# Linear attention in 64-key tiles: the running state takes up a chunk's early keys ahead of its late queries

## The chip, the cores and the metric

The kernel runs on one core of one Trainium2 chip. The metric is the device time of one execution in microseconds (us).

## What is computed

The input is x of shape (16, 512, 256) in float32. Two blocks follow each other, each with a residual. The attention block is causal linear attention with 16 heads of 64 columns:

```python
x = x + attn(layernorm(x))        # Wq, Wk, Wv: 256 x 1024, Wo: 1024 x 256
x = x + ffn(layernorm(x))         # fp4 rounding in blocks of 16 of inputs and weights

q = relu(x @ Wq) + 0.001;  k = relu(x @ Wk) + 0.001;  v = x @ Wv      # per head
context = cumsum(k_n outer v_n)                     # over the positions n, 64 x 64 a head
attn_n = (q_n @ context_n) / (q_n . cumsum(k)_n)
out = attn @ Wo + bo

h = silu(fp4(x) @ fp4(w_gate)) * (fp4(x) @ fp4(w_up));  y = fp4(h) @ fp4(w_down)
```

Since the sum over positions is causal, a block of queries needs the scores q.k of its own block, masked, times v, and q times the state that the keys before the block have left. The denominator comes out of the same products: v has a 65th column of ones.

## The kernel before

A sequence has 4 chunks of 128 tokens, c = 0 to 3; two chunks make a half u. Everything is software-pipelined by chunk: step g = 4b + c handles the attention of chunk g, the gate and up products of chunk g - 2 and the down product of chunk g - 3. Each engine has its queue written out by hand in `step(b, c)`, and engines wait for each other by semaphores only. Heads come in 8 pairs; the heads of a pair lie on partitions 0 to 63 and 64 to 127 of `qkT`. Pairs 0 to 3 are half 0, pairs 4 to 7 half 1.

TensorE's step, in order: in even chunks `turn_x` (transposes of the next half's normalized x); `scores`; `turn_k` (k to token-major, for chunks 0 to 2); `turn_xq`; `project_v` for the next half (six pairs of 512-column matmuls); `attend`; `update_state` (chunks 0 to 2); in odd chunks the first half of `project_qk` for the next half of the sequence, with `turn_hq(0)` and `turn_hq(1)` (transposes of the rounded hidden rows, 4 and 2 of them) between; in even chunks the two `turn_hq` alone; then twice `gate_up` and `turn_attn`; in odd chunks the rest of `project_qk`; `down`; `project_out`.

The projections use float32r operands split in a high and a low part (`product`, L408). The attention products are plain float32, and each shows in the profile as two matmuls. In `scores` the early 64 keys of a pair meet all 128 queries (L473, 64x64 tiles, 128 columns) and the late 64 keys the late 64 queries (L479, 64 columns). In `attend` come the state's products (L514, 64x64, 65 columns, not in chunk 0), early queries by early keys (L527, 64x64) and late queries by all 128 keys (L535, 128x64 tiles). `update_state` (L548) adds the chunk's 128 keys to a pair of PSUM banks (128x64 tiles). Chunk 3 updates no state.

VectorE's step up to the attention: in even chunks `low_x` (L1049, L1075); mask 0 of four (L1188, 128x384 each, scores times the causal mask into `probs`); `variance` of the second layer norm of chunk g - 1, which GpSimd turns to a shift and ScalarE to `xn2` (L849); masks 1 to 3; `begin_x`: amax, scale, inverse and scaled x (L1080 to L1089), which waits for `xn2`; `low_xq`; in odd chunks `round_h(g - 3)` (two ops on 704 columns); `end_x` (L1094, L1096), which waits for ScalarE's square of x; then `normalize(0)` and `normalize(1)` (L1220, L1222), each when its half of the attention is in PSUM; `add_state` (L1208 or L1210), when `update_state` is done; `low_hq`, and so on.

ScalarE's step: in even chunks `high_x`; `xn2` (L849); two evacuations of k to `k_tok` (L854); `xqT_hi` (L838); the square of x (L863); two evacuations of v (L702); then the hidden rows, silu and so on.

The 8 PSUM banks go round. `keys` lists the uses of a period of four chunks in a fixed order; the n-th use gets bank n mod 8, and an entry "none" fills up where an av or kv pair would be split. Ahead of each use, `Banks.take` makes TensorE wait for the semaphore with which the bank's last user's reader let it go: v by `v_ready` (ScalarE's evacuation), av by `attn_ready` (normalization), kv by `state_ready` (the addition of the state), wo by `x2_ready`. The core of it:

```python
spread = []
for key in keys:
    if key[0] in ("av", "kv") and key[2] % 2 == 0 and len(spread) % 8 == 7:
        spread.append(("none", len(spread), 0))
    spread.append(key)
bank_of = {**in_turn(first, 8), **in_turn(spread, 8)}
```

In the first steps the FFN weights are quantized and turned as eight jobs at places of `JOBS_AT`, through banks of `W_BANKS`.

Of the kernel before, what the change touches and what calls it, by code (L numbers as in the profile page):

```python
# [5 lines left out]
ALU = mybir.AluOpType  # L6
# [7 lines left out]
P = 128  # L14
# [40 lines left out]
def build_program(nc, x, Wq, Wk, Wv, Wo, bo, w_gate, w_up, w_down, out):  # L55
# [25 lines left out]
    with ExitStack() as ctx:  # L81
# [37 lines left out]
        probs_banks = sb("probs", [P, 4, 6 * DH])  # L119
# [48 lines left out]
        scores_done, probs_ready = sem("scores_done"), sem("probs_ready")  # L168
        k_turned, k_ready = sem("k_turned"), sem("k_ready")
# [89 lines left out]

        def early_cols(pair):  # L260
            at = pair % 2 * 3 * DH
            return slice(at, at + DH)

        def late_cols(pair):
            at = pair % 2 * 3 * DH + (1 + pair // (PAIRS // 2)) * DH
            return slice(at, at + DH)

# [4 lines left out]
        def key_cols(t, pair, late):  # L272
# [12 lines left out]
                   (1, "project"): (4,), (1, "end"): (5,), (2, "scores"): (6,), (2, "attend"): (7,)}  # L285
# [4 lines left out]
        def first_turn_of(job):  # L290
# [6 lines left out]
        W_BANKS = [("hq", 0, 0), ("hq", 0, 1), ("down", 0, 0), ("xq", 1, 0), ("gate_up", 1, 0), ("down", 1, 0),  # L297
                   ("kv", 2, 0), ("av", 2, 3), ("hq", 2, 0), ("hq", 2, 1)]
# [23 lines left out]
        def flat_slots(t):  # L322
# [3 lines left out]
            (flat_slots(probs_banks[:])[:, 0:INNER], wv_hi[:, 0, :], wv_lo[:, 0, :]),  # L326
# [75 lines left out]
        def _(pe):  # L402
# [53 lines left out]
            def scores(b, c, g, u):  # L456
                t = c % 2
                for n in range(2):
# [33 lines left out]
            def attend(b, c, g, u):  # L492
                pe.wait_ge(v_ready, 4 * (u + 1))
                if c:
                    pe.wait_ge(state_ready, (CHUNKS - 1) * b + c)
# [3 lines left out]
                      for half in range(2)]  # L499
                def dst(pair, odd, late):  # L500
# [3 lines left out]
                if c:  # L504


                    for crossed in (True, False):
                        for j in range(HALF_PAIRS):
                            for odd in range(2):
                                pair = j + HALF_PAIRS * (crossed != (odd == 1))  # L510
                                rows = slice(DH * odd, DH * odd + DH)
                                for late in (False, True):
# [892 lines left out]
```

## Time and profile before

| | |
|---|---|
| median of 3 runs | 1664.71 us (1661.76 to 1668.97) |
| the profiled execution's own time | 1667.57 us |
| its span, first to last instruction | 1665.8 us |
| TensorE matmuls busy | 97% |
| VectorE busy | 68% |
| ScalarE busy | 40% |
| GpSimd busy | 27% |
| mean granted TensorE clock | 0.989 |

Busy time is the union of an engine's instructions. PE is TensorE's matmul side, PEld its weight loads, DVE VectorE, ACT ScalarE, POOL GpSimd. Matmuls overlap, so what a run of them costs is read from its start to the start of what follows it, not from the duration of one.

### The profile page before, as it was taken

How to read it: one execution, taken by the hardware profiler on the slowest of the kernel's cores; microseconds unless marked ns; L12 is line 12 of the kernel's file. 1: busy time of each engine (PE TensorE's matmuls, PEld its weight loads, DVE VectorE, ACT ScalarE, POOL GpSimd, SP SyncE). 2: the span in 40 equal slices, each digit the busy share in tenths (PEclk: the TensorE clock that was granted, in tenths of full speed). 3: DMA queues.
4: the chain of work that ended last, by engine and by line, in shares of the span. 5: the costliest groups of instructions: out<-in, count | busy, mean ns of one | idle time of the engine just before them, and what ended most of it. 6: DMA issues, size and time to landing. Idle time of an engine off the chain costs nothing.

```text
span 1665.8 us, 51272 instructions
## 1 busy us (share of the span) xinstructions
PE 1615.4 (97%) x22436; PEld 1530.2 (92%) x22436; DVE 1130.7 (68%) x2487; ACT 661.8 (40%) x1272; POOL 444.0 (27%) x631
## 2 busy tenths in 40 slices
PE   7889999999999999999999999999999999999976
PEld 6789999999999999999999999999999999999975
DVE  8767666667666667666667767666766666766554
ACT  5333443433444333344343434334344343344321
POOL 3322232222222222233222223222233222223201
PEclk9999999999999999999999999999999999999987
DMA  3100000000000000000000000000000000000000
GB/s 141 43 2 14 9 10 15 11 15 15 14 5 14 12 15 15 15 5 15 14 12 15 15 5 15 14 12 15 15 9 11 14 11 15 15 11 9 8 8 10
DMA packets 21997, 26.55 MB, mean 16 GB/s; under 512 B 1809, under 2 KB 20753, under 8 KB 21777
## 3 DMA queue, kind: packets, MB, share of 16 engines
q1 hardware_dynamic: 21776, 23.27, 4.3%
q8 instruction: 180, 2.95, 0.7%
q14 instruction: 41, 0.33, 0.1%
HBM read 14.88 MB, written 8.39 MB: 14 GB/s over the span
## 4 chain that ended last, share of the span: by engine, by line
PE 93%; DVE 4%; ACT 1%; issue 1%; DMA 1%; POOL 0%; SPq 0%; POOLq 0%; DVEq 0%
PE bank L408 65%; PE bank L535 4%; PE bank L473 4%; PE bank L559 3%; PE bank L514 3%; PE bank L489 3%; PE bank L548 3%; PE bank L599 3%; PE bank L527 2%; PE bank L479 2%; PE bank L577 1%; PE bank L418 1%; DMA qkT<-in_L_attn_Wk 1%; DVE probs L1188 0%; DVE h_amax L1134 0%
## 5 line engine op out<-in xcount | busy, mean ns | idle before, releaser
L976 POOL TENSOR_SCALAR qkT<-qkT 128x512 f32<-128x512 f32 x256 | 188.1, 739 | 317.2 <-ACT qkT L709 317.0
L709 ACT ACTIVATE qkT<-bank 128x512 f32<-128x512 f32 x256 | 152.8, 598 | 292.3 <-PE bank L408 292.3
L408 PE MATMUL bank<-xT_hi,wqk_hi 128*128 128x256 f32 x1024 | 212.6, 289 | 0.6 <-DVE wu_lo L1049 0.6
L408 PE MATMUL bank<-xT_hi,wqk_lo 128*128 128x256 f32 x1024 | 203.7, 280 | 0.0
L408 PE MATMUL bank<-xT_lo,wqk_hi 128*128 128x256 f32 x1024 | 203.5, 280 | 0.0
L1049 DVE TENSOR_TENSOR hqT_lo<-bank,hqT_hi 128x512 fp32r<-128x512 f32 (+1 forms) x128 | 68.2, 555 | 162.0 <-ACT hqT_hi L833 159.3
L995 POOL TENSOR_TENSOR rstd<-var,minus_half 128x1 f32<-128x1 f32 x64 | 35.0, 546 | 474.9 <-DVE var L1237 474.9
L408 PEld LDWEIGHTS bank<-xT_hi,wqk_hi 128*128 128x128 f32 x1024 | 155.9, 189 | 3.4 <-DVE wu_lo L1049 0.8
L408 PEld LDWEIGHTS bank<-xT_hi,wqk_lo 128*128 128x128 f32 x1024 | 156.5, 188 | 0.0
L408 PEld LDWEIGHTS bank<-xT_lo,wqk_hi 128*128 128x128 f32 x1024 | 156.4, 188 | 0.0
L1049 DVE TENSOR_TENSOR attnT_lo<-bank,attnT_hi 128x512 fp32r<-128x512 f32 x128 | 88.4, 692 | 67.7 <-ACT attnT_hi L827 67.7
L1188 DVE TENSOR_TENSOR probs<-bank,causal 128x384 f32<-128x384 f32 x256 | 130.0, 550 | 4.6 <-PE bank L479 3.3
L1250 DVE TENSOR_TENSOR hid<-silu,bank 128x352 f32<-128x352 f32 x128 | 66.8, 521 | 91.0 <-PE bank L408 91.0
L827 ACT ACTIVATE attnT_hi<-bank 128x512 fp32r<-128x512 f32 x128 | 76.3, 598 | 115.5 <-PE bank L559 115.5
L1006 POOL TENSOR_TENSOR xq<-x_scaled,x_scale 128x256 f32<-128x256 f32 x64 | 39.8, 621 | 272.8 <-DVE x_scaled L1096 272.8
L958 POOL TENSOR_TENSOR hq<-h_scaled,h_scale 128x704 f32<-128x704 f32 x64 | 89.0, 1391 | 80.4 <-DVE h_scaled L1096 80.4
L849 ACT ACTIVATE xn<-x,shift,rstd 128x256 f32<-128x256 f32 x63 | 37.9, 602 | 176.9 <-POOL shift L997 176.9
L473 PE MATMUL bank<-qkT 64*64 64x128 f32 x2048 | 95.2, 280 | 4.3 <-issue 1.6
L1094 DVE SCALAR_TENSOR_TENSOR h_scaled<-h_square,h_scaled 128x704 f32<-128x704 bf16 x64 | 61.4, 959 | 50.8 <-ACT h_square L897 50.3
L1222 DVE TENSOR_TENSOR attn<-bank,inv_den 128x512 f32<-128x512 f32 x128 | 88.5, 692 | 4.4
L897 ACT ACTIVATE h_square<-h_scaled 128x704 bf16<-128x704 f32 x62 | 48.8, 787 | 101.1 <-DVE h_scaled L1089 101.1
L408 PE MATMUL bank<-wv_hi,xT_hi 128*128 128x512 f32 x256 | 86.9, 421 | 1.8 <-DVE xT_lo L1049 1.0
(161 smaller groups left out, 3959.7 us busy)
## 6 DMA issues: line engine op xcount, KB each, us to landing
x_in<-in_L_attn_x SPq DMA_DIRECT2D x32, 256.0 KB, 2.8
out<-out_sb SPq DMA_DIRECT2D x64, 128.0 KB, 1.7
qkT<-in_L_attn_Wq SPq DMA_DIRECT2D x1, 1024.0 KB, 8.6
qkT<-in_L_attn_Wk SPq DMA_DIRECT2D x1, 1024.0 KB, 10.7
probs<-in_L_attn_Wv SPq DMA_DIRECT2D x1, 512.0 KB, 3.8
k_tok<-in_L_attn_Wv SPq DMA_DIRECT2D x1, 512.0 KB, 6.1
attn<-in_L_attn_Wo SPq DMA_DIRECT2D x1, 512.0 KB, 11.5
x<-in_L_attn_Wo SPq DMA_DIRECT2D x1, 512.0 KB, 12.3
```

Of the source, the lines that this page charges most:

```text
L408: at = pe.matmul(dst, lhs_at(kt), rhs_at(kt), start=first and kt == 0, stop=last and kt == k_tiles - 1)
L473: pe.matmul(dst, qkT[rows, PAIRS + pair, key_cols(t, pair, False)], qkT[rows, pair, t * P:(t + 1) * P].rearrange("p (a t) -> p a t", t=DH) ...
L535: last = pe.matmul(dst(pair, odd, True), probs_banks[:, j + odd, late_cols(pair)], v[:, c % 2, 2 * pair + odd, :], start=False, stop=True, ...
L709: act.activation(flat(qkT[:, 2 * m:2 * m + 2, :]), bank[bank_of["qk", c, n]][:], ACT.Relu).then_inc(qk_relu, 1)
L827: act.activation(flat(attnT_hi[:, 4 * n:4 * n + 4, :]), flat(turn[bank_of["attn", c, n]][:]), ACT.Copy).then_inc(attnT_hi_ready, 1)
L958: pool.tensor_tensor(blocks(hq[:, 0:FFN], HB), blocks(h_scaled[:], HB), each(h_scale[:], HB), ALU.mult).then_inc(hq_ready, 1)
L976: pool.tensor_scalar(at, at, QK_EPS, 1.0, ALU.add, ALU.mult).then_inc(qk_ready, 1)
L1049: dve.tensor_tensor(dst, src, hi.bitcast(F32), ALU.subtract).then_inc(done, 1)
L1094: dve.scalar_tensor_tensor(scaled, square, SQUARE_SHIFT, scaled, ALU.add, ALU.add).then_inc(chain, 1)
L1188: dve.tensor_tensor(probs_banks[:, n, :].rearrange("p (a t) -> p a t", a=2), bank[bank_of["scores", c, n]][:, 0:6 * DH].rearrange("p (a t) ...
L1222: dve.tensor_tensor(to, got[:, :, :, 0:DH], inv.broadcast_to([P, 2, HALF_PAIRS, DH]), ALU.mult).then_inc(attn_ready, 1)
L1250: dve.tensor_tensor(hid[:, half * FH:(half + 1) * FH], silu[:, half, :], bank[bank_of["gate_up", c, 2 * half + 1]][:, 0:FH], ALU.mult).the ...
```

## The change

For chunks 0 to 2 all attention products become 64x64 tiles. `scores` computes only the two diagonal 64x64 blocks of a head, in two banks instead of four; a new `last_scores` and `last_attend` keep the old form for chunk 3. `attend` now first multiplies the early 64 keys by their values into the kv banks; VectorE's new `add_early` adds this to the state and writes `state_mid`. Then come the probabilities by the values for early and late queries, in two rounds (`first`) with a wait on a new semaphore of TensorE itself, `late_keys_done`, between; then early queries by `state`, late queries by `state_mid`, and last the late 64 keys into the same kv banks (the old `update_state` is gone). VectorE's `add_state` stays as it is.

Beside it: the order of bank turns changes (kv ahead of av, two scores entries instead of four, two entries "spare" in their place that only two of the start-up's weight turns use, after qk 1 in odd chunks and after both hq in even ones); VectorE runs `end_x` and `add_early` ahead of `round_h`; the last weight jobs of the start-up move to later places; GpSimd scales weight job 7 after xq, and ScalarE waits for all jobs in step 2.

```diff
             odd, update = c % 2 == 1, c < CHUNKS - 1
-            keys += [("x", c, 0)] * (not odd) + [("scores", c, n) for n in range(4)]
+            keys += [("x", c, 0)] * (not odd) + [("scores", c, n) for n in range(2 if update else 4)]
             keys += [("k", c, n) for n in range(2) if update] + [("xq", c, 0)]
-            keys += [("v", c, n) for n in range(2)] + [("av", c, n) for n in range(4)]
-            keys += [("kv", c, n) for n in range(2) if update]
+            keys += [("v", c, n) for n in range(2)] + [("kv", c, n) for n in range(2) if update]
+            keys += [("av", c, n) for n in range(4)]
+
+            held = [("spare", c, n) for n in range(2) if update]
             for n in range(2):
-                keys += [("qk", c, 2 * n), ("qk", c, 2 * n + 1)] * odd + [("hq", c, n)]
+                keys += [("qk", c, 2 * n), ("qk", c, 2 * n + 1)] * odd + held * (odd and not n) + [("hq", c, n)]
+            keys += held * (not odd)
...
         JOBS_AT = {(0, "attend"): (0,), (0, "update"): (1,), (0, "end"): (2,), (1, "scores"): (3,),
-                   (1, "project"): (4,), (1, "end"): (5,), (2, "scores"): (6,), (2, "attend"): (7,)}
+                   (1, "project"): (4,), (1, "end"): (5,), (2, "update"): (6,), (2, "end"): (7,)}
...
-        W_BANKS = [("hq", 0, 0), ("hq", 0, 1), ("down", 0, 0), ("xq", 1, 0), ("gate_up", 1, 0), ("down", 1, 0),
-                   ("kv", 2, 0), ("av", 2, 3), ("hq", 2, 0), ("hq", 2, 1)]
+        W_BANKS = [("hq", 0, 0), ("hq", 0, 1), ("gate_up", 0, 2), ("xq", 1, 0), ("gate_up", 1, 0), ("gate_up", 1, 2),
+                   ("hq", 2, 0), ("hq", 2, 1), ("spare", 2, 0), ("spare", 2, 1)]
...
             def scores(b, c, g, u):
+                t = c % 2
+                pe.wait_ge(qk_ready, PAIRS * u + 4)
+                to = [banks.take(pe, ("scores", c, odd), b, probs_ready,
+                                 lambda b, odd=odd: 4 * (CHUNKS * b + c) + 2 * odd + 2) for odd in range(2)]
+                for j in range(HALF_PAIRS):
+                    if j == 2:
+                        pe.wait_ge(qk_ready, PAIRS * (u + 1))
+                    for late in (False, True):
+                        for pair in (j, j + HALF_PAIRS):
+                            at = t * P + late * DH
+                            for odd in range(2):
+                                rows = slice(DH * odd, DH * odd + DH)
+                                cols = probs_cols(pair, 0, late)
+                                last = pe.matmul(bank[to[odd]][key_rows(pair, late), cols],
+                                                 qkT[rows, PAIRS + pair, key_cols(t, pair, late)],
+                                                 qkT[rows, pair, at:at + DH], start=True, stop=True)
+                last.then_inc(scores_done, 4)
...
             def attend(b, c, g, u):
                 pe.wait_ge(v_ready, 4 * (u + 1))
-                if c:
-                    pe.wait_ge(state_ready, (CHUNKS - 1) * b + c)
+                v = v1[c // 2]
+
+                def keys_by_values(k, pair, odd, late):
+                    rows = key_rows(pair, late)
+                    j, at = pair % HALF_PAIRS, pair * P + DH * odd
+                    return pe.matmul(bank[k][DH * odd:DH * odd + DH, j * VW:(j + 1) * VW], k_tok[rows, at:at + DH],
+                                     v[rows, c % 2, 2 * pair + odd, :], start=not late and j == 0, stop=late,
+                                     skip_group_check=True)
+
+
+                pe.wait_ge(k_ready, 2 * ((CHUNKS - 1) * b + c + 1))
+                kv = [banks.take(pe, ("kv", c, n), b, state_ready, lambda b: (CHUNKS - 1) * b + c + 1)
+                      for n in range(2)]
+                for j in range(HALF_PAIRS):
+                    for n in range(2):
+                        for odd in range(2):
+                            last = keys_by_values(kv[n], j + HALF_PAIRS * n, odd, False)
+                last.then_inc(kv_early_done, 1)
+
+                to = [[banks.take(pe, ("av", c, 2 * half + odd), b, attn_ready,
+                                  lambda b, half=half: 2 * (CHUNKS * b + c) + half + 1) for odd in range(2)]
+                      for half in range(2)]
...
+                pe.wait_ge(probs_ready, 4 * g + 4)
+                for first in (True, False):
+                    for half in range(2):
+                        if not first:
+
+                            pe.wait_ge(late_keys_done, 2 * ((CHUNKS - 1) * b + c) + half + 1)
+                        for pair in range(HALF_PAIRS * half, HALF_PAIRS * (half + 1)):
+                            for odd in range(2):
+                                last = probs_by_values(pair, odd, first != (half != odd), first)
+                        if first:
+                            last.then_inc(late_keys_done, 1)
+
+
+                for late in (False, True):
+                    if not late and c == 0:
+                        continue
+                    if late:
+                        pe.wait_ge(state_mid_ready, (CHUNKS - 1) * b + c + 1)
+                    else:
+                        pe.wait_ge(state_ready, (CHUNKS - 1) * b + c)
+                    held = state_mid if late else state[:]
+                    at = c % 2 * P + late * DH
+                    for half in range(2):
+                        for pair in range(HALF_PAIRS * half, HALF_PAIRS * (half + 1)):
+                            for odd in range(2):
+                                rows = slice(DH * odd, DH * odd + DH)
+                                last = pe.matmul(dst(pair, odd, late), qkT[rows, pair, at:at + DH],
+                                                 held[rows, pair, :], start=False, stop=late, skip_group_check=True)
+                        if late:
+                            last.then_inc(av_done, 1)
+
+
+                for j in range(HALF_PAIRS):
+                    for n in range(2):
+                        for odd in range(2):
+                            last = keys_by_values(kv[n], j + HALF_PAIRS * n, odd, True)
+                last.then_inc(kv_done, 1)
...
                 high_ffn_weights(jobs_at(g, "project"))
+                if g == 2:
+
+                    act.wait_ge(ffn_w_quantized, len(ffn_jobs))
...
                 def mask(n):
+                    if c < CHUNKS - 1:
+                        dve.wait_ge(scores_done, 4 * g + 4)
+                        dve.tensor_tensor(probs[:, 512 * n:512 * (n + 1)].rearrange("p (a t) -> p a t", t=DH),
+                                          bank[bank_of["scores", c, n]][:].rearrange("p (a t) -> p a t", t=DH),
+                                          causal[:, 0:DH].rearrange("p (a t) -> p a t", a=1
+                                                                    ).broadcast_to([P, 8, DH]),
+                                          ALU.mult).then_inc(probs_ready, 2)
+                        return
...
+                def add_early():
+                    got = side_by_side("kv", c, 0)
+                    held, mid = (t.rearrange("p (n j) e -> p n (j e)", n=2) for t in (state[:], state_mid))
+                    dve.wait_ge(kv_early_done, (CHUNKS - 1) * b + c + 1)
+                    if c == 0:
+                        dve.tensor_copy(mid, got).then_inc(state_mid_ready, 1)
+                    else:
+                        dve.tensor_tensor(mid, held, got, ALU.add).then_inc(state_mid_ready, 1)
...
                 if now:
-                    for n in range(1, 4):
+                    for n in range(1, 2 if c < CHUNKS - 1 else 4):
                         mask(n)
...
-                if downed and c % 2 == 1 and not last:
-                    round_h(g - 3)
                 if normed:
                     end_x()
                 if last:
                     residual()
+                if now and c < CHUNKS - 1:
+                    add_early()
+                if downed and c % 2 == 1 and not last:
+                    round_h(g - 3)
                 if now:
                     normalize(0)
                     normalize(1)
```

## Rows read from the trace of the kernel before

**Rows 1.** The page: TensorE's busy time, and the chain that ended last.

```profile
PE 1615.4 (97%) x22436; PEld 1530.2 (92%) x22436; DVE 1130.7 (68%) x2487; ACT 661.8 (40%) x1272; POOL 444.0 (27%) x631
...
PE 93%; DVE 4%; ACT 1%; issue 1%; DMA 1%; POOL 0%; SPq 0%; POOLq 0%; DVEq 0%
```

**Rows 2.** Timeline, TensorE, chunk 1's scores: start, length, engine, line, shape, count.

```profile
851.19 0.45 PE L473 MATMUL bank<-qkT 64*64 64x128 f32 x8
851.46 0.29 PE L479 MATMUL bank<-qkT 64*64 64x64 f32 x8
851.58 0.40 PE L473 MATMUL bank<-qkT 64*64 64x128 f32 x8
...
852.69 1.09 PE L489 MATMUL bank<-ident,qkT 128*128 128x128 f32 x8
```

**Rows 3.** Timeline, TensorE, the attention of chunk 0, then of chunk 1.

```profile
838.05 0.70 PE L527 MATMUL bank<-v,probs 64*64 64x65 f32 x32
...
840.69 0.87 PE L599 MATMUL bank<-ident,hq 128*128 128x128 f32 x6
...
856.72 1.16 PE L514 MATMUL bank<-state,qkT 64*64 64x65 f32 x64
857.71 0.65 PE L527 MATMUL bank<-v,probs 64*64 64x65 f32 x32
858.28 1.15 PE L535 MATMUL bank<-v,probs 128*64 128x65 f32 x32
859.27 1.10 PE L548 MATMUL bank<-v,k_tok 128*64 128x65 f32 x32
860.30 0.51 PE L408 MATMUL bank<-xT_hi,wqk_hi 128*128 128x256 f32 x2
```

**Rows 4.** Timeline, VectorE, chunk 2 up to the state; from 852.23, chunk 1.

```profile
787.51 0.42 DVE L1080 TENSOR_REDUCE x_amax<-xn 128x16 f32<-128x256 f32 x1 [0.17 <-ACT xn L849]
...
788.46 0.42 DVE L1089 SCALAR_TENSOR_TENSOR x_scaled<-xn,x_inv 128x256 f32<-128x256 f32 x1
...
789.82 0.42 DVE L1096 SCALAR_TENSOR_TENSOR x_scaled<-x_square,x_scaled 128x256 f32<-128x256 bf16 x1
791.21 0.21 DVE L1220 RECIPROCAL inv_den<-bank 128x8 f32<-128x8 f32 x1 [0.96 <-PE bank L535]
...
792.30 0.69 DVE L1222 TENSOR_TENSOR attn<-bank,inv_den 128x512 f32<-128x512 f32 x1
792.90 0.69 DVE L1210 TENSOR_TENSOR state<-state,bank 128x520 f32<-128x520 f32 x1
...
852.23 0.56 DVE L1188 TENSOR_TENSOR probs<-bank,causal 128x384 f32<-128x384 f32 x1
...
855.64 0.42 DVE L1089 SCALAR_TENSOR_TENSOR x_scaled<-xn,x_inv 128x256 f32<-128x256 f32 x1
```

**Rows 5.** Timeline, ScalarE, chunk 2.

```profile
786.87 0.60 ACT L849 ACTIVATE xn<-x,shift,rstd 128x256 f32<-128x256 f32 x1 [2.33 <-POOL shift L997]
787.38 1.06 ACT L854 ACTIVATE k_tok<-bank 128x512 f32<-128x512 f32 x2
...
789.24 1.06 ACT L702 ACTIVATE v<-bank 128x512 f32<-128x512 f32 x2
```

**Rows 6.** Timeline, TensorE, chunk 2: attention's start, hidden rows' transposes, gate.

```profile
788.92 1.16 PE L514 MATMUL bank<-state,qkT 64*64 64x65 f32 x64
...
792.50 0.88 PE L599 MATMUL bank<-ident,hq 128*128 128x128 f32 x6
793.13 0.57 PE L408 MATMUL bank<-wg_hi,xqT_hi 128*128 128x352 f32 x2
```

**Rows 7.** Timeline, TensorE, start-up, step 2: idle time before a weight turn.

```profile
89.02 0.65 PE L630 MATMUL bank<-ident,hq 128*128 128x128 f32 x2 [3.67 <-ACT k_tok L854]
```

**Rows 8.** Windows: busy time (count) of PE, PEld, DVE, ACT, POOL; granted clock; DMA.

```profile
1574.00:1581.00 7.00, 4.82 (x59) 4.43 (x61) 3.80 (x8) 1.25 (x3) 1.39 (x1) 0.98 0.05 19
1581.00:1585.00 4.00, 4.00 (x62) 3.88 (x55) 3.12 (x11) 1.60 (x3) 0.74 (x2) 0.61 0.01 4
```

More of the change, by code:

```diff
@@ L256, in query_rows, with probs_cols @@
             return slice(at, at + DH)
+        def probs_cols(pair, odd, late):
+            at = 512 * odd + (2 * (pair % (PAIRS // 2)) + late) * DH
+            return slice(at, at + DH)
         def early_cols(pair):
@@ L266, in late_cols @@
             return slice(at, at + DH)
+        probs_banks = probs[:, 0:4 * 6 * DH].rearrange("p (n t) -> p n t", n=4)
+        state_mid = probs[:, 1024:1024 + PAIRS * VW].rearrange("p (n e) -> p n e", e=VW)
         def key_order(pair):
@@ new lines, in dst, with probs_by_values @@
+                def dst(pair, odd, late):
+                    j = pair % HALF_PAIRS
+                    return bank[to[pair // HALF_PAIRS][odd]][query_rows(pair, late), j * VW:(j + 1) * VW]
+                def probs_by_values(pair, odd, late, first):
+                    rows = key_rows(pair, late)
+                    return pe.matmul(dst(pair, odd, late), probs[rows, probs_cols(pair, odd, late)],
+                                     v[rows, c % 2, 2 * pair + odd, :], start=first and pair % HALF_PAIRS < 2,
+                                     stop=False, skip_group_check=True)
@@ L528, in attend @@
                                       v[rows, c % 2, 2 * pair + odd, :],
-                                      start=not c and j == 0, stop=False, skip_group_check=True)
+                                      start=False, stop=False, skip_group_check=True)
                 for half in range(2):
@@ L538, in attend @@
                     last.then_inc(av_done, 1)
-            def update_state(b, c):
-                pe.wait_ge(k_ready, 2 * ((CHUNKS - 1) * b + c + 1))
-                v = v1[c // 2]
-                for n in range(2):
-                    k = banks.take(pe, ("kv", c, n), b, state_ready, lambda b: (CHUNKS - 1) * b + c + 1)
-                    for j in range(HALF_PAIRS):
-                        pair = HALF_PAIRS * n + j
-                        for odd in range(2):
-                            last = pe.matmul(bank[k][DH * odd:DH * odd + DH, j * VW:(j + 1) * VW],
-                                             k_tok[:, pair * P + DH * odd:pair * P + DH * odd + DH],
-                                             v[:, c % 2, 2 * pair + odd, :],
-                                             start=j == 0, stop=True, skip_group_check=True)
-                last.then_inc(kv_done, 1)
             def turn_attn(b, c, g, n):
@@ L659, in step @@
                         project_v(b, c, u + 1, c % 2)
-                    attend(b, c, g, u)
+                    if c < CHUNKS - 1:
+                        attend(b, c, g, u)
+                    else:
+                        last_attend(b, c, g, u)
                 turn_weights(jobs_at(g, "attend"))
-                if now and c < CHUNKS - 1:
-                    update_state(b, c)
                 turn_weights(jobs_at(g, "update"))
@@ L1007, in step @@
                                        ALU.mult).then_inc(xq_ready, 1)
+                    if g == 2:
+                        scale_weights((7,))
                 if c % 2 == 0 and exists(u + 1, ALL_HALVES):
```

45 lines of the change are left out of this document (25 added, 20 removed).

## The prediction

> **What bounds the kernel now.** I read the page's busy shares and its chain first [rows 1]: TensorE is busy 97% of the span and carries 93% of the chain. So every nanosecond of TensorE's queue is on the path, and any new wait in it is added in full. The timeline of one period (chunks 2 and 3 of a sequence, then 0 and 1 of the next) shows TensorE without a gap, so I cost the change in three places: TensorE's own work in `scores` [rows 2] and in the attention part [rows 3], VectorE's queue up to the new addition [rows 4], and ScalarE's evacuations [rows 5], laid beside TensorE in chunk 2 [rows 6]. Chunk 0 repeats chunk 2 here 49.13 us later (first attention product at 838.05 against 788.92 [rows 3, 6]), so rows of chunk 2 serve for both.
>
> **TensorE's prices.** Each float32 product shows as two matmuls. Let g be the time of four 64x64 matmuls on the four quarters of the array, or of two 128x64 ones; s what a run of them loses at its start after another tiling, e what it loses at its end. The starts in chunk 1 [rows 3] give 0.99 = s + 16g (L514, 64 matmuls of 64x64, the same for L535, 32 of 128x64), 0.57 = 8g + e (L527 up to the change to 128x64) and 1.03 = 16g + e (L548 up to 128x128). Hence 8g = 0.46, g = 0.0575, e = 0.11, s = 0.07. Check on chunk 0: 2s + 40g + 2e = 2.66 against 2.64 read. In `scores` two 64-column groups take 0.12 [rows 2], the same g.
>
> The Trainium skill (TensorE: Matmul & The Clock Gate, section "Back-to-back issue gap") says that starts never come closer than about 25 ns, however small the matmul. That speaks against this change, which swaps fewer large matmuls for more small ones. The trace disagrees for quarters used in turn: L514 has 64 in 0.99 us, 15 ns each [rows 3]. The sum below goes by groups; the other way is a rival.
>
> **What it removes and adds, chunk by chunk (waits left aside).**
> `scores`: before 1.50 us (851.19 to 852.69 [rows 2]). After, 64 matmuls of 64 columns, 16 groups: 0.07 + 16 x 0.0575 + 0.11 = 1.10. Saved 0.40, in chunks 0, 1 and 2. I take 0.42, since 64 columns are a touch shorter than 65.
> Attention in chunks 1 and 2: before 56 groups and one more change of tiling, 3.58 (856.72 to 860.30 [rows 3]). After: early keys 8 groups, probabilities 16, state for early queries 8, for late ones 8, late keys 8: 48 groups in one tiling, 0.07 + 2.76 + 0.11 = 2.94. Saved 0.64.
> Attention in chunk 0: 40 groups before and after; one change of tiling goes: 2.64 to 2.48. Saved 0.16.
> Chunk 3 keeps its products. Bare gain: (3 x 0.42 + 2 x 0.64 + 0.16) x 16 = 43 us. The waits decide what is left of it.
>
> **VectorE up to `add_early`.** Two masks of 512 columns replace four of 384. A 384 costs 0.56, a 512 0.69 [rows 4], so the masks get 0.8 us cheaper. But the layer norm's variance stands behind the first mask, and the amax that follows is waiting for ScalarE's xn, itself released by GpSimd's shift [rows 4, 5]. So all that follows comes 0.14 later, and nothing of the 0.8 is seen. Chunk 2: the second rounding op begins at 789.82 + 0.14 = 789.96, lasts 0.42, and the next op may start 0.09 before its end (L1210 behind L1222 [rows 4]): `add_early` 790.30 to 790.99, and with the 0.04 that a release costs (xn ends 787.47, amax starts 787.51 [rows 4, 5]; I take 0.05) the middle state is there at 791.05. Chunk 0: 791.05 + 49.13 = 840.18. Chunk 1: the first mask now waits for all scores. They start at 851.19, end about 852.34, so it starts at 852.38 instead of 852.23; with the 0.14, x_scaled starts at 855.64 + 0.29 = 855.93. Its rounding no longer has `round_h` ahead of it, so it ends as in chunk 2: 1.36 from L1089 to L1096, then 0.34 and 0.69. Middle state at 858.37.
>
> **Chunk 0.** TensorE comes to the attention at 838.05 - 0.42 = 837.63. It now needs k_tok first: ScalarE's ends at 788.44 + 49.13 + 0.14 = 837.71 [rows 5], so 837.76. Early keys take until 838.30, probabilities until 839.25, and the late queries then wait until 840.18, 0.9 us. From there 16 groups: 0.05 + 0.92 + 0.11 to 841.26, against 840.69 before: **0.57 lost**. Queued behind that wait is all of TensorE's step; normalization follows it and is needed only after half of gate_up.
>
> **Chunk 1.** Arrival 856.30, k_tok is there. Early keys to 856.82, probabilities to 857.77, early queries to 858.24, plus 0.1 for the two waits on `late_keys_done`. No row shows such a wait of TensorE on its own matmul: at least 0, as the other half's four groups (0.23) lie between; at most 0.15 each, one drained start (s) and a release. I take 0.05, nearest to s. The middle state at 858.37 is 0.03 late. 858.39 + 1.08 = 859.47 against 860.30: **0.83 gained**. `round_h` and normalization come about 1 us later; the banks av feeds (first used by hq 1.0, 2.9 us on) are free by then.
>
> **Chunk 2** is where bank turns matter. Work out the turn table: v 2.0 and v 2.1 get banks 1 and 2, kv 3 and 4, av 5, 6, 0 and 1, hq 2 and 3. So
> (a) av 2.3 takes v 2.0's bank. ScalarE evacuates v from 789.24 [rows 5], 0.14 later now, the first half done 0.60 on: 789.98. All four av banks are taken ahead of the first probability product, so these start at 790.04 instead of 789.15. Then 0.98 + 0.1 + 0.46: the late queries start at 791.59, past the middle state at 791.05. The attention ends at 791.59 + 1.08 = 792.67, before 792.50 [rows 6].
> (b) hq 2.1 takes kv 2.0's bank, which is free only at `state_ready`. Before, it took v's bank, free since long. `turn_hq` follows the attention at once in this chunk. VectorE: av_done for half 0 at 791.59 + 0.45 = 792.04, then two normalizations and the state addition, 1.69 + 0.69 as at 791.21 to 793.59 [rows 4]: 794.42. TensorE's fifth transpose, due at 793.17, starts at about 794.56 instead of 792.99 before (the six span 792.50 to 793.13 [rows 6]). **1.6 lost**, and behind it stands gate_up with everything else.
>
> **Sum.** 15 x 0.57 - 15 x 0.83 + 14 x 1.6 = +18.5; chunk 2 counts 14 times, since in the last sequence hq is turned ahead of the scores and the first is start-up. Start-up: the 3.67 us wait of a weight turn [rows 7] goes, as job 6 and 7 move behind the attention, with what the low clock after it costs; but in step 1 the weights' bank now stops the whole attention and not only the state's update (24 groups more behind that wait, 1.4 us, partly at the low clock), and job 6 meets wait (b), 1.3. About -2, between -6 and +3. Total +16.5: on the profiled execution's 1667.57 that is 1684; that execution was 2.9 above the median of 1664.71, on which it is **1681 us**.
>
> **Rivals.**
> 1. *hq 2.1's wait does not bind* (VectorE earlier than I make it, or the transposes later). For it: it rests on my reading of the table. Against: 1.25 us would have to go. Chunk 2 then loses 0.15: 15 x (0.57 - 0.83) + 14 x 0.15 - 2 = -4, 1661 us, within measurement. 0.09.
> 2. *No wait costs anything*: 1665 - 43 - 2, so 1620 to 1640 with some left. It ends on the other side. It needs the middle state 0.9 us sooner in chunk 0 and chunk 2's banks free; VectorE's rows say no. It decides faster or not once waits cost under 2.2 us per sequence. 0.07.
> 3. *The clock falls in chunk 2.* Near the end 2.2 us of idle time in 7 is followed by a granted clock of 0.61 over 4 us, against 0.98 [rows 8]: of those 4 us some 3.1 at the lower level, which costs about 1.6, x 15 = 24: 1705 us. Against: my gaps are 0.7 and 1.3, with busy work of 3 us between. 0.06.
> 4. *TensorE pays per instruction.* Attention has 64 matmuls more in chunk 0 and 32 more in 1 and 2, scores as many as before: 128 x 0.031 (L535's price) x 16 = 63 us and the waits, about 1740. This is the skill's 25 ns rule as a mechanism; 15 ns in L514 speaks against it. 0.01.
> 5. *The self-waits cost 0.3 or more each*: 1690 to 1700. 0.05.
>
> **How the numbers follow.** My forecast has 0.72. Its own range: start-up -4/+5, self-waits 0 to 0.15 each in chunks 1 and 2 (-3/+6), release 0.04 to 0.15: 1672 to 1691. The range of 8 in 10 takes a little of rivals 1 and 5: 1669 to 1693. Faster by over 0.5% (about what a measurement here can tell from no change): rival 2 and a part of 1, 0.08. Within 0.5% (1656 to 1673): most of rival 1 and the low edge, 0.10. Slower 0.82.
>
> **What the profile after should show.** `scores` 1.1 us; no 128x64 matmul in chunks 0 to 2. TensorE idle before the late queries in chunk 0, about 0.9, released by `state_mid`'s write; almost none in chunk 1. In chunk 2, idle before the first probability product released by ScalarE's v, and before the fifth hq transpose, released by the state addition, 1.2 to 1.4. No idle before that transpose makes me wrong toward 1661; a step of chunk 2 shorter than before would too; clock below 1.00 in steady state points to rival 3.

## The result

The changed kernel takes 1724.07 us (median of 4 runs, 1722.0 to 1727.06) against 1666.07 for the kernel before on the same chip: ratio 1.035, 95% interval 1.032 to 1.038. It is slower, as forecast, but by 58 us and not by 16, and outside the range.

The page after answers to [rows 1]: TensorE's busy share falls from 97% to 93%, and its share of the chain from 93% to 78%.

```profile
PE 1607.0 (93%) x24484; PEld 1509.5 (88%) x24484; DVE 1135.0 (66%) x2439; ACT 663.8 (39%) x1272; POOL 453.2 (26%) x631
...
PE 78%; DVE 12%; ACT 4%; issue 4%; POOL 1%; DMA 1%; POOLq 0%; SPq 0%; ACTq 0%; DVEq 0%
```

TensorE's work shrank by 8 us though it has 2048 matmuls more; its idle time grew by 64. The chain of waits of TensorE says what ended the idle time (engine, line, waited for: us in total, times, longest). In the kernel after, L533 multiplies keys by values, L557 probabilities by values, L589 the state for the late queries and the late keys, L692 is `turn_hq`, L485 `scores`.

```profile
PE bank L533 <- issue: 15.4, 12, 1.7
PE bank L692 <- DVE state L1326: 13.2, 14, 1.3
PE bank L557 <- ACT v L798: 12.5, 15, 0.8
PE bank L589 <- issue: 11.8, 13, 1.8
...
PE bank L557 <- DVE xqT_lo L1148: 3.7, 16, 0.2
...
PE bank L589 <- DVE probs L1314: 3.0, 16, 0.3
```

Two kinds stand there. Four lines name a semaphore and come 14 to 16 times, once a sequence: those are waits of the order of work. Two lines say "issue", 25 times together, with lengths up to 1.8: TensorE waited for nothing that the profile shows. The timeline of chunk 2 shows the first kind (start, length, engine, line, shape, count, idle time before and its releaser), and answers to [rows 6]:

```profile
1438.19 0.70 PE L533 MATMUL bank<-v,k_tok 64*64 64x65 f32 x32
1439.72 1.26 PE L557 MATMUL bank<-v,probs 64*64 64x65 f32 x64 [0.83 <-ACT v L798]
1440.80 0.65 PE L589 MATMUL bank<-state,qkT 64*64 64x65 f32 x32
...
1442.31 0.66 PE L692 MATMUL bank<-ident,hq 128*128 128x128 f32 x4
1444.27 0.41 PE L692 MATMUL bank<-ident,hq 128*128 128x128 f32 x2 [1.30 <-DVE state L1326]
```

These are (a) and (b) of the prediction. The same view of chunk 0's scores and attention, and of chunk 1's attention, shows the other two waits and a pause of the second kind:

```profile
140.79 1.16 PE L485 MATMUL bank<-qkT 64*64 64x64 f32 x64
141.88 1.10 PE L523 MATMUL bank<-ident,qkT 128*128 128x128 f32 x8
...
146.08 0.70 PE L533 MATMUL bank<-v,k_tok 64*64 64x65 f32 x32
147.01 1.26 PE L557 MATMUL bank<-v,probs 64*64 64x65 f32 x64 [0.23 <-DVE xqT_lo L1148]
148.45 0.70 PE L589 MATMUL bank<-probs,qkT 64*64 64x65 f32 x32 [0.18 <-DVE probs L1314]
...
165.25 0.70 PE L533 MATMUL bank<-v,k_tok 64*64 64x65 f32 x32
166.03 1.26 PE L557 MATMUL bank<-v,probs 64*64 64x65 f32 x64
167.11 0.52 PE L589 MATMUL bank<-state,qkT 64*64 64x65 f32 x20
168.22 0.39 PE L589 MATMUL bank<-state,qkT 64*64 64x65 f32 x11 [0.59 <-issue]
```

Read from start to start, since the ends overlap: L533 to L557 takes 0.93 in chunk 0 and 0.78 in chunk 1, where 0.52 is the least (e8, below), so the wait for `xqT_lo` costs 0.41 and 0.26; L557 to L589 takes 1.44 against 1.08, so the wait for the middle state costs 0.36. The last pause falls in the middle of a run of products with one bank and no wait between them. Counted over TensorE's records (matmuls, weight loads and waits that are instructions), 25 such pauses of 0.38 to 1.76 us stand between 130 and 1600 us, 26.1 us in all, and every one of them comes at the same place of the count: instruction 193 or 194 after a multiple of 256. The kernel before has one there, of 0.59 us, and near the end one of 1.57 at another number. The page's DMA queues explain the 256 (queue, packets, MB, share): before, and then after,

```profile
q8 instruction: 180, 2.95, 0.7%
```

```profile
q8 instruction: 195, 3.19, 0.8%
```

Each of these packets has 16,384 bytes. TensorE has 46,127 records before and 50,143 after (44,872 and 48,968 matmuls and weight loads, the rest waits); 256 to a packet makes 180.2 and 195.9, all of this queue's 180 and 195. So TensorE's instructions come in 16 KB packets of 256. By the trace's times each of the 25 pauses ends 1.2 to 1.6 us after such a packet has landed, 2.2 to 2.9 us after it was asked for. This place is called a packet's end below; why its number is 193, no run shows, and the count starts at the first recorded instruction.

Where that number falls in the work decides. The attention's products of chunk 0 are a run of 322 such instructions, those of chunks 1 and 2 runs of 386. In 14 sequences number 193 falls 36 times among the first 208 instructions of a run, and no such pause stands there; it falls 25 times at instruction 218 of a run or later, and TensorE pauses 23 times. (The other two of the 25 pauses stand in the transposes just behind chunk 0's run.)

The step lengths, from one chunk's scores to the next's, split the 58 us. In us, of the shortest sequence in steady state; the one of the kernel after has no pause:

| | chunk 0 | chunk 1 | chunk 2 | chunk 3 | sum |
|---|---|---|---|---|---|
| before | 18.68 | 31.36 | 19.59 | 29.53 | 99.16 |
| after | 19.34 | 30.78 | 21.39 | 29.62 | 101.13 |
| forecast | +0.57 | -0.83 | +1.60 | 0 | +1.34 |
| measured | +0.66 | -0.58 | +1.80 | +0.09 | +1.97 |

The mean sequence, though, is 103.26 (from 140.79 to 1586.39, 14 of them) against 99.29 before, 3.97 more. So 14 x 1.97 = 27.6 us are regular, and the pauses add 14 x 2.00 = 28. What stands ahead of these sequences takes 3.5 more and what follows them 3.3 less: 55.8 us, the difference of the two profiled spans.

### The profile page after: what moved, and what is told of

The parts are those of the page before. It is cut to its first block, busy times and chain, and to the rows that moved or that the text cites. A ratio compares the mean times of both kernels' runs of the same rounds, so it can differ in the third digit from the quotient of the medians.

```text
span 1721.6 us, 55290 instructions
## 1 busy us (share of the span) xinstructions
PE 1607.0 (93%) x24484; PEld 1509.5 (88%) x24484; DVE 1135.0 (66%) x2439; ACT 663.8 (39%) x1272; POOL 453.2 (26%) x631
## 4 chain that ended last, share of the span: by engine, by line
PE 78%; DVE 12%; ACT 4%; issue 4%; POOL 1%; DMA 1%; POOLq 0%; SPq 0%; ACTq 0%; DVEq 0%
PE bank L423 58%; PE bank L652 3%; PE bank L589 3%; PE bank L557 2%; PE bank L692 2%; PE bank L533 2%; DVE probs L1288 1%; DVE xT_lo L1148 1%; ACT xn L945 1%; PE bank L507 1%; ACT xT_hi L811 1%; PE bank L485 1%; PE bank L622 1%; POOL rstd L1094 1%; PE bank L642 1%
## 5 line engine op out<-in xcount | busy, mean ns | idle before, releaser
L1103 POOL TENSOR_TENSOR xq<-x_scaled,x_scale 128x256 f32<-128x256 f32 x64 | 48.5, 758 | 229.6 <-DVE x_scaled L1195 229.6
L929 ACT ACTIVATE hqT_hi<-bank 128x512 fp32r<-128x512 f32 x122 | 58.0, 488 | 113.9 <-PE bank L692 113.3
L533 PEld LDWEIGHTS bank<-v,k_tok 64*64 64x64 f32 x3072 | 57.6, 135 | 41.2 <-issue 41.1
L533 PE MATMUL bank<-v,k_tok 64*64 64x65 f32 x3072 | 69.0, 223 | 21.0 <-issue 15.4
```

The costliest lines, as they stand in the source:

```text
L533: return pe.matmul(bank[k][DH * odd:DH * odd + DH, j * VW:(j + 1) * VW], k_tok[rows, at:at + DH], v[rows, c % 2, 2 * pair + odd, :], start ...
L929: act.activation(flat(hqT_hi[:, k0:k1, :]), flat(turn[bank_of["hq", c, n]][:, 0:k1 - k0, :]), ACT.Copy).then_inc(hqT_hi_ready, 1)
```

## The experiments

The theories: A, the regular part is the waits (a), (b) and that of chunk 0; B, the irregular part is the supply of TensorE's instructions. All ratios are against the kernel before on the same chip, where it took 1665 to 1667 us.

**e1, the two bank turns apart.** The banks of (a) and (b) are exchanged for ones let go earlier.

```diff
+        bank_of["k", 2, 1], bank_of["v", 2, 0] = bank_of["v", 2, 0], bank_of["k", 2, 1]
+        bank_of["hq", 2, 1], bank_of["gate_up", 2, 1] = 7, 5
```

> The changed kernel with four bank turns of chunk 2 exchanged: k 2.1 and v 2.0 trade banks, hq 2.1 gets bank 7 and gate_up 2.1 bank 5, so that no av or hq use of chunk 2 stands behind v or the state. Theory A (bank turns cost chunk 2 its time): the idle time before the fifth hq transpose (1.30 us, 14 times) and 0.6 of the 0.83 us before the first probability product go, chunk 2's step falls from 21.39 to about 19.5 us, the whole from 1724 to 1696 to 1702. Rival (TensorE's instruction supply is the bound: 25 irregular stalls of 0.4 to 1.8 us without a semaphore, each ending 1.2 to 1.5 us after a 16 KB instruction packet has landed): the waits removed turn partly into such stalls, and the time stays above 1705 us.

1696.64 us, ratio 1.018 (1.016 to 1.019), as expected. Chunk 2's step falls from 21.39 to 19.35; 27 pauses of 25.1 us in all stay. (a) and (b) cost 2.0 us a sequence, about 28 in all.

**e2, the middle state sooner.** In `step`, `add_early` stands ahead of `end_x` (in the last sequence behind it, as it was).

```diff
+                if now and c < CHUNKS - 1 and not last:
+                    add_early()
                 if normed:
                     end_x()
...
-                if now and c < CHUNKS - 1:
+                if last and c < CHUNKS - 1:
                     add_early()
```

> The changed kernel with VectorE's add_early ahead of end_x (behind it, as it was, in the last sequence). Theory A: the middle state comes 0.8 us sooner; only chunk 0 waits for it now, 0.36 us after its bank wait, so 15 times 0.36: 1718 to 1720 us. Rival (the middle state is the price that I forecast, 0.9 us in chunk 0): 1710 us or less.

1721.79, ratio 1.033 (1.031 to 1.034), 2 us above the expected range and by the median alone no clear change. The trace shows it: chunk 0's step is 18.93 for 19.34, 0.4 us, and the pauses, which move, take most of it back (26 of 29.8 us in all).

**e3, both.**

> Both edits. Theory A: sum of the two, 1690 to 1697 us; chunk 0's step about 19.0, chunk 2's 19.5 us where no instruction stall falls in it. What then stays over the 1666 of before is the irregular stalls (2 us a sequence) and start-up. If it lands at 1670 or less, the irregular stalls were a consequence of the waits and not of the instruction supply.

1693.88, ratio 1.016 (1.015 to 1.018), as expected. Steps 18.93, 30.71, 19.34; 26 pauses, 29.6 us. The kernel's regular part is now 0.6 us a sequence below the one before, and it is still 27 us slower. The pauses are of that size.

**e4, the stream shifted.** 32 matmuls of one column at the start, 128 instructions.

```diff
+            for _ in range(32):
+                pe.matmul(bank[7][:, 0:1], ident[:], ident[:, 0:1], start=True, stop=True)
```

> The changed kernel with 32 one-column matmuls ahead of the first transpose, 128 more of TensorE's instructions in a stretch in which it waits for x anyway; all that follows is the same program, only at other places of the instruction stream. Supply theory: in the changed kernel all 26 irregular stalls stand at the same place of the stream, instruction 193 or 194 modulo 256 as the records count; here they again stand at 193 or 194, so at products that are 128 instructions earlier in the work, at none of the old places, and the steps that have one are others (the old sequences with a step of 32.99, 23.46 or 21.12 us change). Total within 12 us of 1724. Rival (the stalls belong to the work, a PSUM or operand conflict of certain 64x64 products): they stay at the same products and sequences, and their place in the stream becomes 65 or 66.

1729.03, ratio 1.037 (1.036 to 1.039). The pauses are again all at 193 or 194 of 256 (22, 21.5 us), now in front of other products and in other sequences. They follow the count and not the code. The time itself tells little, as the first scores come 8.8 us later.

**e5, av banks taken late.** e3 showed that `attend` still waits for `xqT_lo` ahead of all its probability products, as one of the four av banks is the bank of xq. Here half 1's banks are taken just ahead of half 1.

```diff
-                to = [[banks.take(pe, ("av", c, 2 * half + odd), b, attn_ready, ...
+                to = []
...
                     for half in range(2):
+                        if first:
+                            to.append([banks.take(pe, ("av", c, 2 * half + odd), b, attn_ready, ...
```

> e3_both with the av banks of half 1 taken just ahead of half 1's first product instead of together with half 0's. Theory: in each of chunks 0 to 2 the probability products wait for xqT_lo only since half 1 uses xq's bank (0.1 to 0.4 us of idle time, 28 times on the page of the changed kernel); taken 0.25 us later the wait is gone in full or nearly: 0.2 to 0.4 us a chunk, 8 to 14 us, so 1680 to 1686 us, less what the denser stream gives back to the irregular stalls (then 1686 to 1692). Rival (the wait is hidden behind another one): 1692 to 1696 us.

1677.8, ratio 1.008 (1.006 to 1.010), 2 us better than expected. Steps 18.46, 30.47, 18.94, 29.6: a sequence is 97.5 us, 1.7 less than before, and 27 pauses of 29.1 us take it back.

**e6, chunk 0 as before.** e5 with `last_scores`, `last_attend` and a separate update of the state in chunk 0, whose new form saves least: its attention takes 2.69 for 2.64 (e14, below).

> e5 with chunk 0 in the form of the kernel before (three score blocks, 128-row products, update_state behind), chunks 1 and 2 in the new one. Chunk 0's bare step was 18.68 us in the kernel before and 18.9 us in e3, so without irregular stalls this would change little (within 3 us of e5). Supply theory: the old form has half as many instructions per time in its 128-row products, so chunk 0's irregular stalls (some 0.5 us a sequence) go too: 5 to 10 us faster than e5.

1665.7, ratio 0.9995 (0.9985 to 1.0005), 12 us faster than e5 where 5 to 10 were expected. Chunk 0 takes 18.66 every time in steady state; the 21 pauses left (21.8 us) are in chunks 1 and 2.

**e7, the supply by itself.** The kernel before, with 1024 products of 64x64 with 64 columns on the four quarters at its start (each two matmuls and two weight loads), then 512 of 128 columns.

```diff
+            for count, width in ((1024, 64), (512, 128)):
+                for k in range(count):
+                    rows, cols = k % 2 * DH, k // 2 % 2 * DH
+                    pe.matmul(bank[6 + k % 2][cols:cols + DH, 0:width], ident[rows:rows + DH, 0:DH], ...
```

> The kernel before with 1024 float32 products of 64x64 by 64 columns on the four quarters in turn, then 512 of 128 columns, ahead of everything else, their results unused: 4096 and 2048 instructions in a row. Array theory: 512 groups of 0.058 and 256 of 0.110 us, 30 and 28 us. Supply theory: the first run cannot go faster than a 16 KB packet (256 instructions) per 2.2 to 2.9 us, so 16 packets take 35 to 46 us and idle time stands at every 256th instruction; the second run needs 256 instructions per 3.5 us and shows no such idle time. If the first run takes 30 to 31 us without idle time, the supply theory is wrong.

Its one run took 1753.3 us; what counts is the timeline of TensorE:

```profile
21.83 2.09 PE L617 MATMUL bank<-ident 64*64 64x64 f32 x128 [0.27 <-issue]
25.28 2.09 PE L617 MATMUL bank<-ident 64*64 64x64 f32 x128 [1.36 <-issue]
29.01 2.09 PE L617 MATMUL bank<-ident 64*64 64x64 f32 x128 [1.64 <-issue]
32.47 2.09 PE L617 MATMUL bank<-ident 64*64 64x64 f32 x128 [1.36 <-issue]
...
64.92 3.31 PE L617 MATMUL bank<-ident 64*64 64x64 f32 x128 [1.36 <-issue]
68.65 1.58 PE L617 MATMUL bank<-ident 64*64 64x128 f32 x49 [0.41 <-issue]
```

Nothing but independent products, and TensorE stands still after each 128 matmuls, which with their 128 weight loads are 256 instructions. Twelve blocks from 21.83 to 64.92 are 3.59 us each, 71 instructions a us, of which TensorE is busy for 2.09; the granted clock is 1.00 there. In the count these pauses, too, begin at number 193. A packet takes longer than the 2.2 to 2.9 us expected. With 128 columns, twice as long each, two pauses of 0.41 and 0.28 are left in eight packets, where none was expected.

So 3.59 us is what a packet costs when the stretch is all dense. A short stretch may go faster: the kernel before has 320 instructions in the 3.58 us of chunk 1's attention (89 a us), with one pause of 0.59 in 1470 us, at instruction 300 of its run.

**e8 and e9, the packet ends put in place.** If B holds, a kernel whose sequence is a whole number of packets meets their ends always at the same products. e8 is e6 with waits already met, two calls to an instruction, ahead of some products: 70 instructions a sequence, which is then 3072 = 12 x 256 long. (The count of 140 in the expectation is that of the calls.) e9 has 128 such instructions more once, at the start. The expectation has e8's packet ends outside the dense runs; by the traces number 193 lies within them in both kernels, as a run of 386 holds one or two. In e8 it is instruction 162 of chunk 1's run and 195 of chunk 2's, in e9 34 and 290, and 67 and 323.

```diff
                 for kt in range(k_tiles):
+                    more = min(1, pad[0])
+                    pad[0] -= more
+                    for _ in range(2 * more):
+                        pe.wait_ge(constants_ready, 6)
                     at = pe.matmul(dst, ...
...
+                if now:
+                    pad[0] += {1: 55, 3: 15}.get(c, 0)
```

> This is e6 (late taking of the transpose banks, swapped banks, chunk 0 with whole-chunk products) with extra waits on TensorE that are already met, each an instruction of its own: 140 a sequence, so that a sequence is 3072 = 12 x 256 TensorE instructions and every sequence meets the ends of the 16 KB instruction packets at the same places, which are chosen to lie outside the dense attention stretches. Supply theory: the 21 stalls of e6 (21.8 us) go nearly all, the waits cost at most a few us: 1643 to 1652, ratio 0.986 to 0.991. Rival (the stalls hang on something that merely comes along with the dense stretches, a bank or a port): the extra instructions only add, 1666 to 1672.

> As e8, with 128 more met waits once at the start: the same instructions in a sequence, but each packet end now lies half a packet further, inside the dense stretches of chunk 1 and chunk 2 of every sequence. Supply theory: a stall of 0.7 to 1.4 us in both chunks of every sequence, 25 to 38 us over e8: 1670 to 1688. Rival: no difference to e8 beyond what the start-up takes (up to 9 us).

e8: 1647.4, ratio 0.989 (0.987 to 0.991). e9: 1681.23, ratio 1.009 (1.007 to 1.011). The same attention of chunk 1, first in e8 and then in e9:

```profile
1143.15 0.70 PE L542 MATMUL bank<-v,k_tok 64*64 64x65 f32 x32
1143.67 1.22 PE L564 MATMUL bank<-v,probs 64*64 64x65 f32 x64
1144.71 0.64 PE L600 MATMUL bank<-state,qkT 64*64 64x65 f32 x32
1145.18 0.64 PE L600 MATMUL bank<-probs,qkT 64*64 64x65 f32 x32
1145.65 0.64 PE L542 MATMUL bank<-v,k_tok 64*64 64x65 f32 x32
1146.22 0.51 PE L432 MATMUL bank<-xT_hi,wqk_hi 128*128 128x256 f32 x2
```

```profile
1165.50 0.70 PE L542 MATMUL bank<-v,k_tok 64*64 64x65 f32 x32
1166.02 1.22 PE L564 MATMUL bank<-v,probs 64*64 64x65 f32 x64
1167.07 0.64 PE L600 MATMUL bank<-state,qkT 64*64 64x65 f32 x32
1167.53 0.41 PE L600 MATMUL bank<-probs,qkT 64*64 64x65 f32 x16
1169.10 0.40 PE L600 MATMUL bank<-probs,qkT 64*64 64x65 f32 x13 [1.16 <-issue]
```

e9 has 29 pauses at 193 or 194, one in chunk 1 and one in chunk 2 of nearly every sequence, 31.4 us, all at instruction 290 or 323 of the run; e8 has one, of 0.38, behind a run. 34 us between two kernels that differ only in 128 instructions at their start: B is shown. So a packet end in a run does no harm by itself; one that comes late in it does. The border lies near instruction 210: in all these kernels the earliest pause is at 208 of a run (once, in e1), while places up to 199 have none (e8 at 162 and 195, e14 at 146, 168 and 199, in every sequence). What sets it, no run took apart.

**e10 and e11, all chunks in the new form, aligned.** e5 and the changed kernel itself with 199 such instructions a sequence (13 x 256), up to two in a row.

```diff
+                    more = min(2, pad[0])
...
+                    pad[0] += {0: 80, 1: 55, 3: 64}.get(c, 0)
```

> e5 (all products of the change, chunk 0 too, in 64-wide tiles, both banks swapped, late taking) with met waits so that a sequence is 3328 = 13 x 256 instructions, and the packet ends outside the dense stretches. Supply theory: e5's 27 stalls (29.1 us) go, the waits give a few us back: 1648 to 1658, ratio 0.989 to 0.995, so the finer products come out ahead of the kernel before. Rival: 1678 to 1686.

> The changed kernel itself, its banks and its order untouched, with the same met waits as e10. Supply theory: it loses its 28 us of supply stalls and keeps the semaphore waits: 1694 to 1704, ratio 1.017 to 1.023. That would split the change's +58 us into about 28 us of supply and 30 us of waits. Rival (the supply stalls hide behind waits that would be there anyway): 1715 to 1726.

1793.74, ratio 1.077 (1.074 to 1.079), and 1847.15, ratio 1.109 (1.106 to 1.112): both far off. The pauses are gone, but each step with pads is 3 us longer (e10: 21.9, 33.6, 18.9, 33.0). The pads (the waits already met) themselves cost, which e8 had hardly shown.

**e12 and e14, the same with at most one ahead of a product; e13, e8's ahead of wide products only.**

```diff
-                    more = min(2, pad[0])
+                    more = min(1, pad[0])
```

```diff
-                    more = min(1, pad[0])
+                    more = min(1, pad[0]) if dst.shape[-1] >= 300 else 0
```

> e11 again, the changed kernel with its banks and order untouched and 199 met waits a sequence (3328 = 13 x 256 instructions), but at most one of them ahead of a product and not two. e11 took 1847, and it had no supply stall longer than 0.35 us in the dense stretches: its own waits cost about 10 us a sequence, with two of them ahead of a product in a row. Theory: a met wait ahead of each product costs about 0.011 us (e8: chunk 1 with 55 of them took 31.1 us where 30.5 is the shortest without), so about 2.2 us a sequence, 34 in all; the supply stalls of 28 us go: 1706 to 1732, with chunk 0's step about 20.2, chunk 1's 31.4, chunk 2's 21.4 and chunk 3's 30.3, all alike over the sequences. Rival (the regular steps of e11 came from the alignment itself and not from the waits): 1830 to 1850 again.

> e10 again (e5 with the change's products in every chunk, a sequence of 13 x 256 instructions) with at most one met wait ahead of a product. e5 took 1677.8 with 29 us of supply stalls; they go, and the 199 waits cost about 34: 1662 to 1690, with every sequence alike. Rival as in e12: about 1790 again.

> e8 with the same 70 met waits a sequence, but only ahead of products of 352 or 512 columns, which last long enough to cover one. Theory: e8's chunk 1 gives its 0.6 us back, 16 times: 1636 to 1642, ratio 0.983 to 0.987. Rival (a met wait costs the same wherever it stands): 1646 to 1649 as e8.

e12: 1703.97, ratio 1.022 (1.020 to 1.024). e14: 1650.07, ratio 0.990 (0.988 to 0.992), 12 us under the expected range. e13: **1639.9**, ratio 0.983 (0.981 to 0.985), the best of all and 27 us under the kernel before. In e12 no pause of 0.35 is left between 130 and 1600 us, and the mean sequence is 101.97 us: 1.29 less than in the changed kernel, 0.84 more than its one sequence without a pause. So the pads, 2.2 us a sequence by the expectation, cost 0.84, nearly all in chunk 1; 14 x 1.29 = 18 of the 20 us that e12 gains on the changed kernel. What stays there is the regular part, in the chain of waits of e12:

```profile
PE bank L697 <- DVE state L1333: 18.2, 14, 1.3
PE bank L562 <- ACT v L805: 12.5, 15, 0.8
```

The 13.2 us of (b) in the changed kernel were 18.2, then: in some sequences a pause just ahead had hidden it.

In e14, scores and attention of chunk 0, then of chunk 2:

```profile
236.86 1.16 PE L492 MATMUL bank<-qkT 64*64 64x64 f32 x64
237.96 1.09 PE L530 MATMUL bank<-ident,qkT 128*128 128x128 f32 x8
...
242.15 0.70 PE L540 MATMUL bank<-v,k_tok 64*64 64x65 f32 x32
...
244.84 0.88 PE L701 MATMUL bank<-ident,hq 128*128 128x128 f32 x6
...
286.36 1.16 PE L492 MATMUL bank<-qkT 64*64 64x64 f32 x64
287.45 1.09 PE L530 MATMUL bank<-ident,qkT 128*128 128x128 f32 x8
...
291.65 0.70 PE L540 MATMUL bank<-v,k_tok 64*64 64x65 f32 x32
...
294.72 0.87 PE L701 MATMUL bank<-ident,hq 128*128 128x128 f32 x6
```

## Why the forecast failed, step by step

**TensorE's prices: the failed step.** "The sum below goes by groups" took 0.0575 us for four small matmuls wherever they stand. As a price that was right: chunk 0's scores take 1.09 (forecast 1.10), chunk 1's attention without a pause 3.07 (1143.15 to 1146.22 in e8; forecast 2.94 and 0.1 of self-waits). What failed was to take it for a price that holds however long a run is. L514's 64 matmuls in 0.99 us are 128 instructions, half a packet; the change makes runs of 192 matmuls, 384 instructions in 3.07 us, 125 a us, where e7 sustains 71. Whenever the end of a packet falls late enough in such a run, from about instruction 210 on, TensorE stands still. This is 28 of the 58 us, a term that the sum did not have. The waits, 27.6 us net of what the products save, had 18.5 in the forecast: they give its direction, but not the size measured.

**Rival 4** (TensorE pays per instruction) had 0.01 and named the right resource with the wrong law. It would have given about 1740 and a price on every matmul; the runs show none as long as the packets keep up, and then a pause at one place in 256. One row of a short run could not rule out a limit that only long runs meet; e7 could. The Trainium skill (TensorE: Matmul & The Clock Gate, section "Back-to-back issue gap") puts its floor at about 25 ns a matmul. Here e7's blocks come to 28 ns a matmul over a long run (3.59 us by 128), and L514's 15 ns stand for a short one, so neither number alone describes it.

**Chunk 0: +0.66 for 0.57.** The size was near by luck, the split was not. `attend` waits 0.23 for the bank of xq, which I had missed, 0.41 by its effect, so that only 0.36 of the 0.9 is left ahead of the late queries; the waits come to less than forecast, and the 0.16 that I took for saved products is not there (below); e2 and e5 took 0.41 and 0.47 off this step.

**Chunk 1: -0.58 for -0.83.** The same wait for the xq bank makes the 0.25 of difference (0.26 by the starts; e5 takes 0.24 to 0.31 off). The self-waits on `late_keys_done` are small, as taken: 3.07 without a pause, by 2.94 for the products, leaves about 0.13 for both.

**Chunk 2: +1.80 for +1.60.** Both waits are at the places and with the releasers forecast: (a) 0.83 by ScalarE's v (0.89 forecast), (b) 1.30 by the state's addition (1.4). e1 took 2.04 away by banks alone. Rivals 1 and 2 are out with it. Late taking gave another 0.4 in this chunk.

**Start-up: -2 forecast, +3.5 measured** up to the scores of the second sequence (140.79 against 137.25; the first three steps are 23.05, 34.74, 24.11 against 19.22, 33.18, 25.67). That is the wrong sign and just outside the bound of +3; the last sequence, for which the forecast has -0.3, gave 3.3 back. No run took either apart.

**Rival 3**, the clock: granted 0.988 for the whole against 0.989, full in steady state through gaps of 0.83 and 1.30. Out. **Rival 5**, self-waits of 0.3: out, as above.

**The bare gain of 43 us.** Without waits and pauses (e14) the scores take 1.10 and 1.09 in chunks 0 and 2, the attention 3.07 in chunk 2 for 3.58 and 2.69 in chunk 0 for 2.64: 0.41 x 3 + 0.51 x 2 - 0.05 = 2.2 us a sequence, 35 us of the 43. Chunk 0 saves nothing in its attention, where I had 0.16. The steps of e5 show 99.16 - 97.47 = 1.7 of the 2.2; the other 0.5 lies outside the products that I costed, and was not traced.

## What to carry to other kernels

Before you replace large matmuls by small ones, count the instructions in the longest run without a long product, and set it against what the supply of the engine sustains: here 256 every 3.6 us, where e7's products on the four quarters keep TensorE busy for 2.1. If pauses named "issue" appear, number the instructions modulo 256; if they all fall on one number, suspect the supply, as here. Then a few instructions more or fewer in a period of the kernel can put that number where long products, or the first 190 instructions or so of a run, stand under it. And take a PSUM bank just ahead of the product that writes it: four taken together wait for the last of four readers.

## What the runs showed that was not expected

A shift of 128 instructions at the very start changed the whole kernel's time by 34 us, 2% (e8, e9), though both kernels have packet ends within their dense runs; only how late in the run they come differs. So a version of such a kernel is only fairly judged when the places of its packet ends are known.

A wait already met is not always free. e8's 55 in chunk 1, nearly all ahead of products of 256 columns, make that step 31.24 us at the median where 30.47 is the shortest without them, 0.014 for each. With most of them moved to products of 352 or 512 columns it is 30.73 (e13), and chunk 2, which then carries some 30 of them, takes 18.94, where 18.84 is the shortest without. The width alone does not give the price, though: e12's 80 in chunk 0, some 30 of them ahead of 256 columns, cost nothing (19.33 for 19.34). Two in a row made each step with pads 3.1 to 3.4 us longer (e10 against e5; 28 to 40 products carry them, so 0.09 to 0.11 for each). Why the second costs so much more was not found.
